# Two residuals moved ahead of three results on VectorE, a root regrouped on POOL, and a flag summed and converted earlier

## The reference, cut to what matters

```
h  = relu(layernorm(x))
s  = act_quant(relu(act_quant(h) @ weight_quant(weight)))     # 4-bit activations, 3-bit weights
x1 = x + adj @ s                                              # with the scales folded in
h2 = relu(layernorm(x1))
out = x1 + (attention factor) @ h2
```

## Time and profile before

| what | value |
|---|---|
| median of 3 runs | 140.11 us (139.88 to 144.45) |
| the profiled execution's own time | 140.66 us |
| its span | 138.9 us |
| granted TensorE clock, mean | 0.973 |
| busy: PE, PEld, DVE, ACT, POOL | 116.0, 69.9, 113.3, 96.3, 70.6 us |
| TensorE matmuls | 554 |
| bytes moved | 32.44 MB, mean 234 GB/s |

### The profile page before, as it was taken

One profiled execution on the slowest core, in us unless ns is written; L12 is line 12 of the kernel. 1 busy time (PEld: TensorE's weight loads), 2 busy tenths in 40 slices (PEclk: granted clock), 3 DMA queues, 4 the chain that ended last, 5 costly groups with the idle time before them and its releaser, 6 DMA issues.

```text
span 138.9 us, 1928 instructions
## 1 busy us (share of the span) xinstructions
PE 116.0 (83%) x554; PEld 69.9 (50%) x558; DVE 113.3 (82%) x249; ACT 96.3 (69%) x145; POOL 70.6 (51%) x104
## 2 busy tenths in 40 slices
PE   0299999979976999999999999999999999985000
PEld 0295545534533455545757575757567485564000
DVE  0789999679969987977999999999499993799930
ACT  3678787775779989739999979896098898430200
POOL 2464533416823655970000689978978878121310
PEclk9999999999999999999999999999999999999955
DMA  4999999997799999999883897157162542422140
GB/s 128 346 419 367 409 416 391 295 226 188 224 227 303 262 193 364 378 420 350 292 323 28 328 421 270 38 185 249 42 206 80 187 134 76 157 107 84 70 151 12
DMA packets 18289, 32.44 MB, mean 234 GB/s; under 512 B 7842, under 2 KB 10659, under 8 KB 16739
## 3 DMA queue, kind: packets, MB, share of 16 engines
q1 hardware_dynamic: 15730, 24.29, 52.4%
q10 hardware_dynamic: 1584, 5.64, 12.6%
q0 software_dynamic: 960, 2.36, 5.9%
HBM read 24.66 MB, written 6.30 MB: 223 GB/s over the span
## 4 chain that ended last, share of the span: by engine, by line
POOL 35%; issue 20%; DVE 14%; ACT 10%; PE 7%; DMA 3%; ACTq 0%; DVEq 0%; POOLq 0%
POOL narrow L836 12%; POOL raw L824 9%; POOL rs L743 5%; POOL lo L755 5%; PE acc L1361 4%; DVE st L1015 3%; ACT junk L540 3%; DMA h_iT<-h_i 3%; ACT z_sup L567 3%; ACT h_i L559 2%; ACT hi L525 2%; DVE ring L1122 2%; DVE x_sb L1260 1%; PE acc L1374 1%; PE acc L1379 1%
## 5 line engine op out<-in xcount | busy, mean ns | idle before, releaser
L1434 PE MATMUL acc<-sup,lo 128*128 128x512 f32 x128 | 32.0, 402 | 0.0
L1428 PE MATMUL acc<-sup_h,hi 128*128 128x512 f16 x128 | 29.0, 380 | 0.0
L1434 PEld LDWEIGHTS acc<-sup,lo 128*128 128x128 f32 x128 | 24.0, 188 | 5.7
L540 ACT ACTIVATE junk<-raw,below 128x2048 uint8<-128x2048 f32 x12 | 23.9, 1993 | 0.4
L1379 PE MATMUL acc<-sup,lo 128*128 128x512 f32 x64 | 21.5, 447 | 0.3 <-DVE sup L1060 0.3
L824 POOL DMA_INDIRECT raw<-adj_g,at_sb x12 | 11.9, 991 | 18.0 <-DMA at_sb<-at_d 15.0
L1015 DVE BATCH_NORM_STATS2 st<-x_sb 128x6 f32<-128x512 f32 x29 | 19.4, 685 | 0.4
L1428 PEld LDWEIGHTS acc<-sup_h,hi 128*128 128x128 f16 x128 | 11.9, 98 | 15.4 <-issue 2.2
L836 POOL DMA_INDIRECT narrow<-sup_d,at_sb x12 | 17.4, 1446 | 3.7 <-issue 3.7
L743 POOL TENSOR_TENSOR rs<-ve,minus_half 128x2 f32<-128x2 f32 (+3 forms) x16 | 14.3, 895 | 9.3 <-DVE ve L1025 9.1
L1361 PE MATMUL acc<-w_q,h_qT 128*128 128x512 bf16 x60 | 15.7, 381 | 3.3 <-DVE h_qT L1055 2.8
(11 more groups left out here) (117 smaller groups left out, 153.5 us busy)
## 6 DMA issues: line engine op xcount, KB each, us to landing
raw<-adj_t SPq DMA_DIRECT2D x11, 1024.0 KB, 5.4
raw<-adj_t ACTq DMA_DIRECT2D x8, 512.0 KB, 5.5
out<-ring SPq DMA_DIRECT2D x15, 256.0 KB
x_sb<-x SPq DMA_DIRECT2D x3, 1024.0 KB, 14.2
sup_d<-sup_h SPq DMA_DIRECT2D x4, 512.0 KB
w_sb<-weight SPq DMA_DIRECT2D x4, 258.0 KB, 3.9
raw<-adj_t ACTq DMA_DIRECT2D x1, 1024.0 KB, 5.3
x_sb<-x SPq DMA_DIRECT2D x1, 512.0 KB, 5.8
```

The costliest lines, as they stand in the source:

```text
L540: nc.scalar.activation(junk[:, :], raw[:, k % RAW, :], ACT.Relu, bias=below[:, :], accum_out=screen[:, k:k + 1]).then_inc(screened, 1)
L1428: nc.tensor.matmul(bank[:, cols], part(hi, k % PARTS, j), sup_h[:, j, cols], start=(j == 0), stop=False)
L1434: ins = nc.tensor.matmul(bank[:, cols], part(lo, k % PARTS, j), sup[:, j, cols], start=False, stop=(j == T - 1))
```

## The change

Four edits:

1. VectorE's order: residual 12, residual 13 and split_rest(3) now come directly after split_lo of tile 14, and results 9 to 11 after them, followed by count_row as before.
2. POOL's roots: the entries for tiles 8 and 9 to 11 become entries for tiles 8 to 9 and 10 to 11. The first is taken before the gathers of tile 15, the second after them.
3. TensorE sums the flag between the two halves of tile 15 rather than after them. The sum waits for the row counts, and the matmuls of the second half are queued behind it.
4. VectorE converts the flag in the last residual, after the statistics of the first half and ahead of the second half, rather than after the last result. All engines' reads of the flag wait for this conversion.

```diff
-        second_roots = [(0, GT), (4, 4), (8, 1), (9, 3)] + [(t, 1) for t in range(12, T)]
+        second_roots = [(0, GT), (4, 4), (8, 2), (10, 2)] + [(t, 1) for t in range(12, T)]
...
                         step(nc.vector.tensor_scalar(st[:, t, 2:3], st[:, t, 2:3], float(D) * EPS, None, ALU.add))
+                        dve.wait_ge(flag_sum, 1)
+                        nc.vector.tensor_copy(flag[:, :], acc[0][:, 0:1]).then_inc(flag_ready, 1)
...
             split_lo(ordinal(14))
+            residual(12)
+            residual(13)
+            split_rest(3)
             result(9)
             result(10)
             result(11)
-            residual(12)
-            residual(13)
-            split_rest(3)
             count_row()
...
             last_result(T - 1)
-            dve.wait_ge(flag_sum, 1)
-            nc.vector.tensor_copy(flag[:, :], acc[0][:, 0:1]).then_inc(flag_ready, 1)
...
+            def sum_flags():
+
+                pe.wait_ge(row_counted, 1)
+                pe.wait_ge(x1_ready, 9)
+                nc.tensor.matmul(acc[0][:, 0:1], ones[:, :], ones_row[:, 1:2], start=True, stop=True).then_inc(flag_sum, 1)
...
                     if t == T - 1 and cols is halves[1]:
+                        sum_flags()
                         pe.wait_ge(x1_ready, T - 2)
...
-            pe.wait_ge(row_counted, 1)
-            pe.wait_ge(x1_ready, 9)
-            nc.tensor.matmul(acc[0][:, 0:1], ones[:, :], ones_row[:, 1:2], start=True, stop=True).then_inc(flag_sum, 1)
```

## The result

The changed kernel takes 0.9644 of the time of the kernel before, 95% interval 0.9583 to 0.9705, over runs of both on one chip: 3.6% faster. I had forecast 136.0 us, a ratio of 0.971. Two later timings of the same pair gave 0.978 and 0.967, so by time alone the gain is 2.2 to 3.6% from one timing to another.

The account below looks back on a forecast made before the run. VectorE's order, with a 3.10 us wait for POOL, and the flag-started tail set the end; 2.8 us from earlier T plus 1.3 from the tail gave 4.1, so median 136.0 us, range 135.2 to 136.9 (8 in 10: 134.5 to 137.6).

Parts of the forecast that it names:

- The gap of 3.10 and its filling: VectorE's 3.10 us wait for POOL's roots of tiles 9 to 11, filled by moved work; residual 14 3.0 us earlier.
- the list: Forecast VectorE times from 115.70: residuals to 119.29, split 119.97, results 9 to 11 121.97, counting 122.88, results 12 and 13 124.21.
- What comes next, TensorE and ScalarE at once: Before residual 14, VectorE meets TensorE (tile 14 done 124.13) and ScalarE's tile 13 copy, waiting for tile 9's ring place (122.9).
- The quarter of the way up: Tile 9's store acknowledged at 122.9, a quarter of the way between bounds 122.3 and 124.85.
- upper bound: Latest acknowledgement of tile 9's store: 4.1 us from issue, as the last store took, so 124.85.
- The flag's sum and conversion: TensorE's sum, 0.28 us or 0.0, hidden by 0.7; VectorE's conversion adds 0.15 before the last half result.
- The tail: From last half result to span's end: 5.6 us before, forecast 4.25 set by VectorE's drain, 1.3 gained.
- T: The end of the last half result on VectorE: 133.33 before, forecast 130.5.
- Rival 1: After the last half result, code fetches were slow only together; spread out, end at T + 2.6 to T + 3.2; chance 0.13.
- Rival 2: Flag's part does nothing: last store and VectorE's fetch collide, tail stays 5.6 us, span 137.3; chance 0.10.
- Rival 3: Tile 9's ring store takes until 124.85, delaying tile 13's copy and result; 1.9 us lost, 137.9; chance 0.11.
- Rival 4: POOL locked out by VectorE, remaining roots take 2.82 us each; slower, span 139.6, time 140.8; chance 0.06.

Follow-up runs that it names:

- result13_late: Changed kernel with result 13 behind the residual of tile 14 instead of in front; one run, no ratio, split to residual 14 10.77 us, then 6.78 to T.
- count_first: Changed kernel with the counting of the row ahead of results 9 to 11 instead of behind them; ratio to the kernel before 0.975.
- flag_only: Kernel before with only the flag summed between the halves and converted inside the last residual, old order and root entries kept; ratio to before 0.992.
- order_only: Kernel before with only the new VectorE order and new root entries, flag left at the end; ratio to before 0.991.

## Why the prediction was right, point by point

- **The gap of 3.10 and its filling**: as forecast, with every start that the trace shows within 0.2 of the list (results 9 to 11 at 6.39 after the split, forecast 6.55; residual 14 at 10.74, forecast 10.9). The order gave 3.15 where I said 3.0.
- **What comes next, TensorE and ScalarE at once**: right on both. result13_late shows TensorE's bound, count_first the ring's; my estimate of 0.6 us for the acknowledgement of a store, on which it hung, gave 122.9 for a store issued at 120.75, 2.15 later, and the trace has 2.1. The quarter of the way up was a guess that came out well. Its upper bound was read slightly low: the last store took 4.24 us from issue, not 4.1.
- **The flag's sum and conversion**: the sum hid, as said. The conversion costs 0.07 of VectorE's time and not 0.15, as flag_only and order_only show (6.09 against 6.03).
- **The tail**: forecast T + 4.25, set by VectorE; it is T + 3.3 to 3.55. This is the mis-sized term: 0.8 of the 1 us by which I fell short (4.1 forecast, 5.1 by the stretches: 3.15 - 0.07 + 2.0). That the time came out at my 136.0 us is luck: the gain was larger than I said, and the ratio of 0.971 that I had forecast lies at the upper end of the first interval. The step that failed says of VectorE that "it reads the flag only after T". The read ran beside the last halves, from 134.5 to 135.3 with T at 135.35, and its row is one of the engine's queue. From today's row I had taken 3.8 us from the read to the drain; only the 3.0 to 3.3 from the branch to the drain stand behind T.
- **Rival 1**, that fetches were slow only in a crowd: false for the engines. TensorE's branch, now alone, still takes 3.57 us against 4.34, and VectorE's way from its branch to its drain stays at 3.0 to 3.3 (2.9 before). It was right in part for the store, which met fewer fetches and fell from 4.2 to 2.6 to 2.9. The end that it gave, T + 2.6 to T + 3.2, is nearer to the T + 3.3 to 3.55 measured than my T + 4.25. **Rival 2**, that the flag does nothing: false, 2 us. **Rival 3**, the ring: the place of tile 9 was free 2.1 us after its store's issue and not 4.1, so nothing was lost; count_first shows that there was no slack. **Rival 4**, POOL, did not occur: the roots of tiles 10 and 11 and of tile 12 took 1.25 together and that of 13 took 0.93, as before, beside residuals, the split and the results (below).

```profile
122.92 1.25 POOL L743 TENSOR_TENSOR rs<-ve,minus_half 128x2 f32<-128x2 f32 x2
124.47 0.93 POOL L743 TENSOR_TENSOR rs<-ve,minus_half 128x1 f32<-128x1 f32 x1 [0.30 <-DVE ve L1025]
```

The Trainium skill (Runtime: NRT & Kernel Launch, Instruction fetch mechanics) has a taken branch out of the fetched window wait for a DMA. The traces agree for two engines: TensorE and VectorE stand for 2.9 to 4.4 us, and in the changed kernel a fetch of code starts 1.0 to 1.1 us after the branch of either. ScalarE and POOL take the same kind of branch and reach their drains 0.2 and 0.5 us later, for which no run here shows the reason. The Trainium skill (SBUF — State Buffer, The DMA setup-cost knee) gives each transfer about 2 us that do not scale with its bytes, and the bytes' time on top. Here a store of 256 KB is done 2.1 us after its issue, bytes included, and one of 128 KB 1.74 without fetches beside it; the measurement decides. With 0.73 us for the bytes of 256 KB and half of it for 128 KB, as in the prediction, the fixed part is about 1.4 in both, an estimate.

## What to carry to other kernels

When an engine with a list written by hand waits for a late operand, put in front of the wait the work whose inputs are already there, and then ask which other engine you have caught up with: here TensorE and the output ring were both reached at once, and the two further reorderings that were tried lose 0.7 and 1 us. A decision that every engine must read at the end should be ready before the last result, since the branch over code that is never run cost 3 to 4 us on two engines here (TensorE and VectorE), and that can lie beside work. Place it by the slowest chain behind the decision, and look in the trace whether an engine's read of the flag can run beside its last instructions, as VectorE's did here.

## What the runs showed of the hardware that was not expected

A jump over a large part that is not executed took 3.4 to 4.3 us on TensorE and 2.9 to 3.3 on VectorE from branch to next instruction, under 0.5 us on ScalarE and POOL, and none of it shows as busy time. The last store, 128 KB, took 1.74 us when no such jump was near and 4.2 when four engines had just jumped.
